# Edge sums of a graph layer: the high and the low rows of a gathered tile side by side in one 512-column product

## The reference

```python
xn = _layernorm(x)
msg = xn[src] * edge_weight[:, None]
seg = edge_type * N + dst                      # 8 relations
h = segment_sum(msg, seg) / maximum(segment_sum(ones, seg), 1)[:, None]
gnn = einsum('rnc,rco->no', h.reshape(8, N, C), weight) + xn @ root + bias
q, k = elu(xn @ wq + bq) + 1, elu(xn @ wk + bk) + 1      # 8 heads of 32
kv, k_sum = einsum('lhd,lhe->hde', k, xn @ wv + bv), k.sum(0)
mix = (einsum('lhd,hde->lhe', q, kv) / (q . k_sum + 1e-06)) @ wo + bo
x = x + gnn + mix
f = _layernorm(x)
probs = softmax(relu(f @ r_w1 + r_b1) @ r_w2 + r_b2)     # 6 experts
top_w, top_i = top_k(probs, 2);  g = softmax(top_w)
x = x + sum over the two chosen e of g_e * (relu(relu(f @ w1[e] + b1[e]) @ w2[e] + b2[e]) @ w3[e] + b3[e])
```

## Time and profile before

| | |
|---|---|
| time of the runs, median | 3180.59 us |
| profiled execution, first to last instruction | 3900.9 us |
| TensorE matmul | busy 3132.7 us, 80% |
| VectorE | busy 2360.3 us, 61% |
| ScalarE | busy 2004.5 us, 51% |
| GpSimd | busy 1638.6 us, 42% |
| mean granted TensorE clock | 0.894 |
| DMA | 456.72 MB, mean 117 GB/s |

### The profile page before, as it was taken

How to read it: one execution, slowest core, us unless ns; L and a number is a source line. 1 busy time by engine, 2 the same in 40 slices (tenths; PEclk the granted TensorE clock), 3 DMA queues, 4 the chain that set the end, 5 groups by cost and what they waited for, 6 DMA issues and landing times.

```text
span 3900.9 us, 48061 instructions
## 1 busy us (share of the span) xinstructions
PE 3132.7 (80%) x16807; PEld 2709.1 (69%) x16808; DVE 2360.3 (61%) x5405; ACT 2004.5 (51%) x3996; POOL 1638.6 (42%) x1696
## 2 busy tenths in 40 slices
PE   6999999766878778777777777787787778787788
PEld 5888887656767767666666667676676667677677
DVE  4497552246666667566666656666565666666675
ACT  3555555334555555454555555555555455545564
POOL 0000000145555555554555555554545455555540
PEclk9999999888888888888889888888888889898899
DMA  6665555543233333233323333233323333233320
GB/s 242 250 259 196 210 210 212 224 144 112 84 93 95 99 96 94 82 94 91 90 77 96 95 92 89 85 97 89 92 83 91 90 93 91 79 97 93 100 67 11
DMA packets 179841, 456.72 MB, mean 117 GB/s; under 512 B 46604, under 2 KB 104918, under 8 KB 159405
## 3 DMA queue, kind: packets, MB, share of 16 engines
q0 software_dynamic: 80352, 219.14, 19.5%
q1 hardware_dynamic: 97074, 232.64, 16.5%
q10 hardware_dynamic: 2172, 1.85, 0.1%
HBM read 296.01 MB, written 158.29 MB: 116 GB/s over the span
## 4 chain that ended last, share of the span: by engine, by line
PE 41%; another core or an unknown queue 12%; DVE 10%; ACT 10%; issue 7%; DVEq 1%; DMA 0%; SPq 0%; ACTq 0%
PE bank L1655 27%; PE acc L1709 7%; DVE row_lo L1394 4%; ACT row_hi L1216 4%; ACT bank L1231 3%; ACT h_hi L1230 2%; PE acc L1718 1%; PE bank L1793 1%; PE bank L1682 1%; PE bank L1691 1%; PE acc L1655 1%; DVE y L1540 1%; DVE h_lo L1473 1%; DVE sel L1388 1%
## 5 line engine op out<-in xcount | busy, mean ns | idle before, releaser
L1159 POOL DMA_INDIRECT ring<-y_tab,tab x1666 | 1624.1, 975 | 1401.6 <-PE acc L1709 869.9
L1230 ACT ACTIVATE h_hi<-bank,bias_t 128x512 fp32r<-128x512 f32 (+1 forms) x600 | 408.9, 682 | 1078.1 <-remote 565.1
L1709 PE MATMUL acc<-row_hi,sel 128*128 128x256 f32 x1666 | 501.6, 329 | 446.5 <-DVE row_lo L1394 255.5
L1709 PEld LDWEIGHTS acc<-row_hi,sel 128*128 128x128 f32 x1666 | 369.9, 222 | 508.3 <-DVE row_lo L1394 291.1
L1216 ACT ACTIVATE row_hi<-ring,tab 128x256 fp32r<-128x256 f32 x1666 | 704.1, 510 | 31.4 <-PE acc L1709 19.4
L1394 DVE SCALAR_TENSOR_TENSOR row_lo<-ring,tab,row_hi 128x256 fp32r<-128x256 f32 x1666 | 685.1, 479 | 48.9 <-ACT row_hi L1216 34.4
L1473 DVE TENSOR_TENSOR h_lo<-bank,h_hi 128x512 fp32r<-128x512 f32 (+1 forms) x600 | 392.6, 676 | 447.2 <-ACT bank L1231 360.5
L790 PE MATMUL yb<-wr_hi,xhl 128*128 128x512 f32 x1568 | 510.9, 398 | 31.5 <-ACT yst L351 25.4
L1655 PE MATMUL bank<-ew_hi,h_hi 128*128 128x256 f32 x1176 | 384.2, 327 | 179.0 <-DVE h_lo L1473 177.7
L1709 PE MATMUL acc<-row_lo,sel 128*128 128x256 f32 x1666 | 480.9, 315 | 13.4 <-issue 13.2
L1540 DVE SCALAR_TENSOR_TENSOR y<-bank,gate,y 128x256 f32<-128x256 f32 x490 | 213.0, 479 | 349.7 <-PE bank L1655 227.7
(11 more groups left out here) (272 smaller groups left out, 5219.7 us busy)
## 6 DMA issues: line engine op xcount, KB each, us to landing
y_tab<-yst SPq DMA_DIRECT2D x97, 1024.0 KB, 3.9
ring<-y_tab,tab POOLq DMA_INDIRECT x1666
xt_tab<-xhl SPq DMA_DIRECT2D x25, 1024.0 KB, 3.9
xc<-xt_tab SPq DMA_DIRECT2D x25, 1024.0 KB
x<-x_tab SPq DMA_DIRECT2D x49, 256.0 KB
xs<-in_x SPq DMA_DIRECT2D x24, 512.0 KB, 6.0
x_tab<-xs SPq DMA_DIRECT2D x24, 512.0 KB, 5.0
out<-y SPq DMA_DIRECT2D x24, 512.0 KB
```

The source lines that it names most:

```text
L1159: pool.indirect_dma_start(out=out_ap, out_offset=None, in_=y_tab[:, :], in_offset=bass.IndirectOffsetOnAxis(ap=idx_ap, axis=0)).then_inc(s ...
L1230: act.activation(dest[:, m, 0:W], b[:, 0:W], ACT.Relu, bias=bias)
L1709: last = pe.matmul(sums(t), sel[:, p % BUFS, q, :], half, start=False, stop=False, skip_group_check=True)
```

## The change

- **Edges.** `row_hi` and `row_lo` become one buffer `halves`, [128, 2 buffers, 6 edge tiles, 2 parts, 256]. One product of 512 columns for each edge tile adds the high rows into one half of a bank and the low rows into the other. A tile's sums take a whole bank, `acc` four banks; VectorE adds both halves to x, one after the other. The root product is brought into the same form: `wqr` holds both parts of the weights side by side, so two products of 256 become one of 512, and the third stays.
- **Banks.** Four for `acc`, four for all other items instead of five. The ramp goes from PSUM to SBUF: `one_hot` reads `iota_w`.
- **Ring.** Four slots instead of six, and GpSimd waits for `lo_ready` (VectorE has split the portion) instead of `portion_used`.
- **Order.** No portion between h2 and h1. `AHEAD_W3` lists one or two portions ahead of each w3, and all are split whole, one after the other, in the order of `SPLIT_AT`. Portion 1 is added behind the first hidden layer, portion 2 ahead of the first w3.
- **Turn of the lap.** TensorE does `close_sum` ahead of the last w3; VectorE adds the sums and forms the statistics (`sums_and_statistics`) ahead of the last y of the lap before.
- **Last biases.** The gates are laid out three times over 96 rows (high, high, low) and the biases (high, low, high) so that one fp32r product of 256 columns a tile does what an fp32 product with 6 rows did. VectorE writes `gate3` with two copies and a subtraction.

The diff, cut to its core:

```diff
-SLOTS, BUFS = 6, 2
+SLOTS, BUFS = 4, 2
+GROWS, GH = 96, 32
-AHEAD_W3 = {0: 3, 1: 4, 2: 6, 3: 8, 4: 10, 5: 11}
-BEHIND_H2 = {2: 5, 3: 7, 4: 9}
+AHEAD_W3 = {0: (2,), 1: (3, 4), 2: (5, 6), 3: (7, 8), 4: (9, 10), 5: (11,)}
+SPLIT_AT = {0: (3, 4), 1: (5, 6), 2: (7, 8), 3: (9, 10), 4: (11, PARTS), 5: (PARTS + 1,)}
...
-            acc = psum(pc, "acc", (P, SUB * C))
-            NBANK = 5
+            acc = psum(pc, "acc", (P, SUB * 2 * C))
+            NBANK = 4
...
-            ramp = psum(pc, "ramp")
             def sums(t):
-                return acc[:, t * C:(t + 1) * C]
+                return acc[:, 2 * t * C:2 * (t + 1) * C]
...
-                    pool.wait_ge(portion_used, portions_before(n, p) - SLOTS + 1)
+                    if nth_portion(n, p) >= SLOTS:
+                        pool.wait_ge(lo_ready, nth_portion(n, p) - SLOTS + 1)
...
-                            if more and e in BEHIND_H2 and AHEAD_W3[e] < parts(i + 1):
-                                high(i + 1, AHEAD_W3[e], 3 * m, 3 * m + 3)
...
-                        if more and between(e + 1) < parts(i + 1):
-                            high(i + 1, between(e + 1))
+                        for p in SPLIT_AT[e] if more else ():
+                            high(i + 1, p)
...
-                    dve.tensor_tensor(sel[:, p % BUFS, 0:size, :], ramp[:, 0:P].unsqueeze(1).to_broadcast([P, size, NT]),
+                    dve.tensor_tensor(hot_r[:, p % BUFS, 0:size, :], iota_w[:, :].unsqueeze(1).to_broadcast([P, size, NT]),
...
+                    for h in range(2):
+                        dve.tensor_copy(gate3[:, 0:T, h * GH:h * GH + 8], gate[:, 0:T, :])
+                    dve.drain()
+                    dve.tensor_tensor(gate3[:, 0:T, 2 * GH:2 * GH + 8], gate[:, 0:T, :], gate3[:, 0:T, 0:8].bitcast(F32),
+                                      ALU.subtract).then_inc(gate_ready, 1)
...
+                def sums_and_statistics(i, T):
+                    dve.wait_ge(x1_in, 32 * (i + 1) if i < SUPER - 1 else 32 * i + 16)
+                    for h in range(T // 2):
+                        dve.wait_ge(acc_full, 2 * i + h + 1)
+                        two = slice(2 * h, 2 * h + 2)
+                        dve.tensor_tensor(x1[:, two, :], acc_parts[:, two, 0, :], x1[:, two, :], ALU.add)
+                        dve.drain()
+                        dve.tensor_tensor(x1[:, two, :], acc_parts[:, two, 1, :], x1[:, two, :], ALU.add).then_inc(x1_done, 1)
...
                         for h in range(T // 2):
-                            if h == 1 and coming is not None and e + 1 in BEHIND_H2:
-                                low_rows(i + 1, coming)
                             b = take(i, plan, "w3", (e, h))
...
+                            if h == 0 and len(coming) == 2:
+                                low_rows(i + 1, coming[0])
+                                one_hot(i + 1, coming[1])
...
                     for q, (t, k) in enumerate(tiles_of_portion(p)):
-                        for half in (row_hi[:, p % BUFS, q, :], row_lo[:, p % SLOTS, q, :]):
-                            last = pe.matmul(sums(t), sel[:, p % BUFS, q, :], half, start=False, stop=False,
-                                             skip_group_check=True)
+                        last = pe.matmul(sums(t), hot_r[:, p % BUFS, q, :], halves[:, p % BUFS, q, :, :], start=False, stop=False,
+                                         skip_group_check=True)
...
                         hidden("h2", e)
-                        if more and BEHIND_H2.get(e, PARTS) < parts(i + 1):
-                            aggregate(i + 1, BEHIND_H2[e])
                         hidden("h1", e + 1)
...
-                        if more and AHEAD_W3[e] < parts(i + 1):
-                            aggregate(i + 1, AHEAD_W3[e])
+                        for p in AHEAD_W3[e] if more else ():
+                            aggregate(i + 1, p)
+                        if more and e == EXPERTS - 1:
+                            close_sum(i, plan)
```

196 lines of the change are left out of this document (101 added, 95 removed).

## The result

The changed kernel takes 3222.2 us (median of 4 runs, 3218.3 to 3227.9) against 3181.6 us before on the same chip: ratio 1.0129, interval 1.0103 to 1.0154. It is slower by 1.3%. The forecast was 3150 us.

The account below looks back on a forecast made before the run. TensorE's 85 us plus 6.1 us of waits was taken to fill the 91.2 us lap. After: 83.1 + 6.6 = 89.7 for 91.1, 24 x 1.4 = 34 less, some 3 more in the first group: 3150 us, range 3125 to 3175.

Parts of the forecast that it names:

- One-hots from SBUF: GpSimd's gathers beside one-hots with two SBUF inputs: 0.8 us a lap added, giving 87.5, under the lap.
- My upper end, 3.9: One-hots' cost to GpSimd if one gather in eight waits half a one-hot: 3.9 us a lap.
- The base: GpSimd's lap without the one-hots' added cost: 68 gathers at 0.975 + 0.30 us, 86.7 us.
- Rival C: GpSimd becomes the bound by its one-hots: 86.7 + 3.9 = 90.6 us, 3180 us, no change; chance 0.14.
- The bias term: Last biases' product on TensorE in fp32r over 96 rows: 1.92 us becomes 0.5, 1.4 less a lap.
- The wide product: Edges on TensorE: 68 products of 512 columns for 136 of 256, saving 0.5 to 0.7 us a lap, 0.4 taken.
- My waits of 6.6: TensorE's waits in the new lap, mainly for VectorE's y and h_lo in experts 1 and 2: 6.5 to 6.7 us.
- 83.1: TensorE's own work a lap after the change, down 1.9 us from 85.0.
- Rival A: VectorE and banks idle TensorE at expert 2's h1 and denominators, halving its clock: lap 92.6, 3220 us; chance 0.32.
- Rival B: TensorE's waits fall to 1 or 2 us, GpSimd's 87.5 us lap becomes the floor: 3094 us; chance 0.18.
- The ring of four: Gather slots freed by low rows: nothing in the laps, 2 us once in the first group.
- The doubled sums: VectorE adds two more tensors at the lap's end: 1.6 us, covered by queries and root product.

Follow-up runs that it names:

- e5: Kernel before with only the bias product changed, to fp32r over 96 rows: 33 us less, lap 91.50 us.
- e9: Kernel before with the changed kernel's order and the fp32r bias, keeping two 256-column products, five banks, ramp in PSUM and ring of six: 3091.3 us.
- e15: Kernel e9 with three gathers and one plain transfer a portion instead of five or six gathers: lap 86.4 us.
- e12: Kernel e9 with one line changed, the one-hots reading their ramp from SBUF: 4.0 us a lap and 89 us in all slower than e9.
- e3: Changed kernel with three gathers and one plain transfer a portion instead of five or six gathers: 3143.6 us.
- e6: Changed kernel with one-hots by tensor_scalar per tile and the low rows' subtraction replaced by a scaled copy: 3136.1 us.
- e1: Kernel before with the one-hots compared with the ramp in SBUF instead of PSUM: no change in time, profiled span 3187.4 us.
- e10: Kernel before with the ramp in SBUF, four ring slots freed when low rows are made, and low rows in their own buffers: no change in time.
- e8: Changed kernel's layout and fp32r bias with the order of the kernel before: 3213.9 us.
- e2: Changed kernel with one-hots written one tile at a time by tensor_scalar, one SBUF operand: 3231 us.
- e11: Changed kernel with the ramp back in a PSUM bank, leaving three banks instead of four for the rest: 3407.7 us.

## Why the prediction was wrong

**The laps, one part at a time.** Before 93.1; bias in fp32r 91.5 (e5); new order 88.6, TensorE alone 86.4 (e9, e15); ramp in SBUF 92.65 (e12); the rest of the layout 94.0, TensorE alone 90.6 (after, e3). Two good parts are worth 4.5 us a lap, and what makes room for the wide product takes 5.3 back.

**The step that failed is "One-hots from SBUF. ... I take 0.8: 87.5, still under the lap".** They cost 3.8 us a lap (4.0 by e12). My upper end, 3.9, was right almost to the digit, and I set it aside for the value nearest to a mean. (That it fits so well is in part the stretch: from 1000 to 3000 us it is 3.4.) That mean came from gathers beside low rows in a trace whose laps were 121 us long, where GpSimd idled, its issue aside, for 30% of the time ((1200 - 638 - 659 x 0.3) / 1200): 14 gathers a lap started in low rows, against 19 in the kernel after, and they were held 0.11 us each against 0.28. The base failed with it: 68 x 0.975 held 2 us of holds in low rows, the changed kernel has 5.3, most of the rise by the new order (2.4 in e5, 4.8 in e9). So GpSimd's lap is 84.7 + 5.3 + 3.8, not 87.5. Rival C named this mechanism and its two signs (gathers over 1.02 us, GpSimd's waits near zero), both of which came. It ended at no change because it too rested on 86.7, and it had a chance of 0.14.

**TensorE's side was near, for a reason only half right.** With GpSimd's bound away the changed kernel takes 3143.6 us (e3) or 3136.1 (e6), where I forecast 3150, and its lap 90.6 to 91.0 for 89.7. The bias term held (1.6 for 1.4). The wide product runs at the pace I gave it. One portion of twelve products in the kernel after, and the next instruction:

```profile
1561.70 2.93 PE L1729 MATMUL acc<-halves,hot_r 128*128 128x512 f32 x12
1564.47 0.28 PE L1671 MATMUL bank<-ew_hi,h_hi 128*128 128x256 f32 x1
```

(1564.47 - 1561.70) / 12 = 0.231 us, against 2 x 0.118 to 0.12 in the earlier trace rows, so 0.3 to 0.6 us a lap, as priced. My waits of 6.6 were 5.6; the rest of the lap was 85.0, where I had 83.1. But I treated them as the price of the new order. They are the price of four banks and the doubled sums for the most part: in the same order without these TensorE waits 1.8 us behind y and 2.1 in all (e15). I never priced the layout against the order without it, so I did not see that the part with 0.5 us of gain asked for a bank, for the ramp's bank and for a second addition of the sums.

**Rival A** (half clock behind long waits, 92.6) gave the time, 3220, but another cause made it. Its mechanism is there all the same, where it was placed. The kernel after, the second half of h1 of expert 2, the denominators and expert 1's two portions; then the stretch at the end of them, with the granted clock as third from last:

```profile
1798.02 0.51 PE L1671 MATMUL bank<-ft_hi,ew_hi 128*128 128x512 f32 x1 [2.38 <-DVE y L1551]
1800.99 1.95 PE L1701 MATMUL bank<-ksum_h,qf 128*128 128x4 f32 x16 [1.32 <-DVE h_lo L1511]
1802.80 4.55 PE L1729 MATMUL acc<-halves,hot_r 128*128 128x512 f32 x12
```

```profile
1803.90:1807.30 3.40, 3.40 (x10) 2.50 (x9) 1.31 (x2) 0.00 (x0) 2.73 (x3) 0.50 0.30 88
```

Behind waits of 2.4 and 1.3 us TensorE ran at 1.2 GHz for 3.4 us, and the twelve products took 4.55 us where those of 1561.70 took 2.93. I had argued that waits of 3 us or less would not do this. With GpSimd as the bound it costs nothing here. In e3, where TensorE is the bound, 5.2 us of a lap are at half clock, in e15 3.4, in e6 9.3, in e1 4.2 (from the granted clock over the loop). If TensorE is busy all through such a stretch it loses half of it: an estimate of 2.6 us a lap in e3, 1.7 in e15 and 2.1 in e1. So of e3's 85.0 us some 82.4 are work at full clock, where I had 83.1; of e15's 84.3 it is 82.6, and of e1's 87.3 it is 85.2, where I had 85. By this estimate my sums of the instructions held, and what I left out was the clock, in the kernel before too.

**Rival B** (waits go, GpSimd's floor rules) is nearest to e9, 3091 for 3094, but that is another kernel, without the layout, and its holds are not those that B assumed.

**Smaller steps.** The lap before was 93.1, not 91.2: I read the part ahead of the laps from the disturbed execution, and TensorE took some 87 us, not 85 (93.1 less the 5.8 that e1 shows of waits). The waits themselves were read rightly: the 2.0 us that I worked out for low rows is 2.1 at most in e1, and the 4.13 of the earlier trace rows belongs to the disturbed lap. The first lap starts 10 us later, where I had 3 us; with the two edits of e6 it starts at 912.1 again. The ring of four, priced at nothing: no time where TensorE bounds (e10), some 0.016 us on a gather. The doubled sums put nothing in front of the queries, in the new order: TensorE waits 7 us for xn_c in 2000 (31 in the old order, e8).

**What stays open.** The 42 us between e12 and after are the wide product with the low rows beside the high ones, the four banks, the doubled sums and the ring of four together. e3 and e15 show that these cost TensorE 4.2 us a lap, hidden when GpSimd bounds; e10 suggests the ring for the 1.3 us a lap that is seen, which was not tried by itself in the new order. Why one gather 0.42 us into a block is held to its end and another not is open as well: with a one-hot starting 0.36 to 0.38 us into the gather there are some of 2.13 us and some of 0.95.

## What to carry to other kernels

Before a change, work out the floor of the engine that generates the gathers from what one costs alone (0.945 + 0.30 us here), and add every VectorE instruction with two SBUF operands as something that can hold it; a mean out of a trace where that engine idles is not a price for a kernel in which it does not. Give each part of a change its own line and ask what it takes from the others: here 0.5 us of matmul was bought with two PSUM banks, of which one, with the doubled sums, covered 3.5 us of waits and the other 4 us of holds. The version to keep is e9, order and bias without the layout, 3091 us.

## What the runs showed of the hardware

- A gather is held by VectorE instructions with two SBUF operands, `tensor_tensor` with a comparison among them, up to the end of one instruction (1.75 us at a one-hot of 0.95) or through a whole run of them (2.86 us in six low rows of 0.41). With drains of 0.14 us between them no gather that started in low rows took over 1.20 us. VectorE's instructions are not lengthened by gathers (0.951 for 0.947 us).
- The same section of the Trainium skill says that `tensor_tensor` with both inputs in SBUF contends with GpSimd's reads, and infers that it does not stall descriptor generation, which would need the write side. These gathers read their row numbers from SBUF (`tab`), so the first sentence covers them: e1 and e12 have 3.1 and 3.6 us of holds a lap in one-hots, e9 with the ramp in PSUM none. Which access it is that waits, no run tells.
- The one-hot by `tensor_scalar` over 128 columns, one SBUF operand, hardly holds a gather (1.17 us at most in e2, 1000 to 3000 us). Over 256 columns, in e6, six in a row held some: 2.02 us for the gather at 1665.77, which started 0.17 us ahead of them, 2.14 at most, and these are most of the 3.0 us a lap that are left. So one SBUF operand is not always enough.
- Taking holds away in one place can bring them back in another: e2 took 3.5 us a lap from the one-hots and got 3.6 in the low rows. It need not: e9 has none in the one-hots and in the low rows what e12 has (4.8 and 4.9).
- TensorE fell to half clock behind waits of 2.4 and 1.3 us, and twelve products of 512 columns took 4.55 us for 2.93.
- A PSUM bank less cost more than any of this: from four to three banks the lap rose to 101.8 us (e11).
